# A decoder layer with expert choice: the threshold search split by batch, and the experts in a new order

## The reference

```
probs = softmax(einsum('bsd,ed->bse', x, choice_w), axis=-1)     # 8 experts
G, I = top_k(swapaxes(probs, -1, -2), k)                         # k = 256 of 1024 tokens
x_in = take_along_axis(x[:, None, :, :], I[..., None], axis=2)
h = silu(einsum('bekd,edf->bekf', x_in, w1))
x_mlp = einsum('bekf,efd->bekd', h, w2)
out[b, I] += G[..., None] * x_mlp      # then layernorm(x + out)
```

## Time and profile before

| | us |
| --- | --- |
| median of 3 runs | 1949.45 |
| lowest, highest | 1948.77, 1952.26 |
| the profiled execution's own time | 1959.72 |
| its span | 1957.9 |
| PE busy | 1668.1 |
| DVE busy | 1134.5 |
| ACT busy | 891.8 |
| POOL busy | 429.8 |

### The profile page before, as it was taken

The page is one execution under the profiler, slowest core; times in us unless marked ns, Lnnn a source line. Parts: engine busy times, 40 slices in busy tenths (PEclk is TensorE's granted clock), DMA queues, the critical chain, the costliest instruction groups (busy, mean ns, idle before and its releaser), DMA issues. The chain is left out here.

```text
span 1957.9 us, 32981 instructions
## 1 busy us (share of the span) xinstructions
PE 1668.1 (85%) x10632; PEld 848.3 (43%) x10632; DVE 1134.5 (58%) x1939; ACT 891.8 (46%) x1585; POOL 429.8 (22%) x547
## 2 busy tenths in 40 slices
PE   6599988798999888989998798999967844999993
PEld 3033334444332445433324354333245433888883
DVE  5577725756777256567763665677435366333424
ACT  2077773342777534347774343577833300111112
POOL 5200004302000052020001611100031001555563
PEclk9599999897999988979998899799988955999997
DMA  6700003622000044220000632200003040335446
GB/s 187 163 2 1 2 25 87 163 48 71 2 2 2 27 127 134 49 59 2 2 2 27 164 98 53 54 2 2 2 21 78 2 150 28 75 77 107 77 89 193
DMA packets 98037, 120.07 MB, mean 61 GB/s; under 512 B 17180, under 2 KB 73500, under 8 KB 97820
## 3 DMA queue, kind: packets, MB, share of 16 engines
q1 hardware_dynamic: 85468, 97.13, 18.1%
q0 software_dynamic: 12416, 20.98, 5.7%
HBM read 80.30 MB, written 40.79 MB: 62 GB/s over the span
## 5 line engine op out<-in xcount | busy, mean ns | idle before, releaser
L881 ACT ACTIVATE pT<-banks 128x512 f32<-128x512 f32 x1184 | 645.2, 596 | 254.8 <-PE banks L1492 150.0
L1034 DVE TENSOR_REDUCE nmf<-banks 128x1 f32<-128x1024 f32 x512 | 606.0, 1220 | 173.5 <-PE banks L1442 171.6
L1492 PE MATMUL banks<-qst,kst 99*128 99x512 bf16 x1024 | 344.0, 388 | 12.1 <-DVE nmf L1034 6.3
L1442 PE MATMUL banks<-kst,qst 96*128 96x512 bf16 x1024 | 327.0, 404 | 31.9 <-DMA kst<-k_parts 21.8
L1524 PE MATMUL banks<-pT,V 128*32 128x512 f32 x2048 | 273.8, 606 | 20.6 <-ACT oT L872 14.0
L1492 PEld LDWEIGHTS banks<-qst,kst 99*128 99x128 bf16 x1024 | 96.0, 97 | 307.2 <-ACT pT L881 185.8
L703 POOL CAST nmp<-nmf 128x16 bf16<-128x16 f32 x64 | 12.7, 198 | 831.4 <-DVE nmf L1034 516.6
L944 ACT ACTIVATE kst<-banks 128x512 f32<-128x512 f32 x64 | 38.2, 597 | 287.0 <-PE banks L1747 278.6
L1442 PEld LDWEIGHTS banks<-kst,qst 96*128 96x128 bf16 x1024 | 98.6, 100 | 146.4 <-DVE nmf L1034 37.3
L1029 DVE TENSOR_REDUCE nmf<-banks 128x4 f32<-128x616 f32 x128 | 99.6, 797 | 86.6 <-PE banks L1436 79.7
L1053 DVE RECIPROCAL rz<-banks 128x16 f32<-128x16 f32 x64 | 16.1, 251 | 204.5 <-PE banks L1552 203.4
(11 more groups left out here) (176 smaller groups left out, 2016.7 us busy)
## 6 DMA issues: line engine op xcount, KB each, us to landing
qst<-q_parts SPq DMA_DIRECT2D x48, 256.0 KB, 5.2
kst<-k_parts SPq DMA_DIRECT2D x48, 256.0 KB, 3.8
qst<-in_w SPq DMA_DIRECT2D x16, 512.0 KB
q_parts<-kst SPq DMA_DIRECT2D x48, 128.0 KB, 2.5
k_parts<-kst SPq DMA_DIRECT2D x48, 128.0 KB, 3.9
qx_parts<-kst SPq DMA_DIRECT2D x48, 128.0 KB, 3.1
qxs<-qx_parts SPq DMA_DIRECT2D x24, 256.0 KB, 5.0
qst<-qx_parts SPq DMA_DIRECT2D x24, 256.0 KB, 4.9
```

The costliest lines, as they stand in the source:

```text
L881: act.activation(pT[:, n % RING_P, :], PS[:, banks[what, n], :], ACT.Exp, scale=scale).then_inc(s_ex, 1)
L1034: dve.tensor_reduce(nmf[:, m % 2, j, t:t + 1], scores.rearrange("p a n -> p (a n)"), AX.X, ALU.max, negate=True).then_inc(s_smu, 1)
L1442: ins = pe.matmul(pair[:, half, :], qst[0:KQ, h, t * P:(t + 1) * P], kst[0:KQ, h, half * N:(half + 1) * N], start=True, stop=True)
L1492: ins = pe.matmul(ps, kst[0:KM, head, kc * P:(kc + 1) * P], qst[0:KM, head, cols], start=True, stop=True)
```

## The change

The search now belongs to a batch (8 columns instead of 32) and takes 3 bits in a turn, so 10 turns with 7 candidates each; a turn has one compare 448 wide, one product of PE with 448 columns (`count`), a reduction of it over the tiles from PSUM into `counts`, and the test and maximum as before. For batches 0 to 2 the ten counts stand in the tail of the next self-attention, one behind every fourth `st`; PSUM bank 3 is theirs, and the tail's scores have six banks instead of seven. In batch 3, `route_early` makes marks, ranks, the first three one-hots and the first tokens for the three batches between the first layernorm and cross-attention, while PE has the two rank steps among its query products and three picks behind them. POOL issues the first three gathers (six DMAs) behind the first `split_max` group of that cross-attention; three more picks stand in its tail. Weights 0 and 1 are loaded in that cross-attention.

The units are then: 24 for batches 0 to 2 (n = 3e + b), in whose first 12 the fourth batch's search and ranks are done, one step a unit; and 8 for batch 3, one expert each. There are three slots instead of four for gathered rows and results, so POOL issues gather n + 3 and scatter n; four weight buffers, with 16 loads instead of 8; `pick` and `choose` are six units ahead. The loops over experts are written out. SP stores each batch's layernorm twice, into `x2_rows` and `acc_rows`, and the four copies by POOL go. Sums of batches 0 to 2 are loaded from unit 24 on and their layernorms stand among units 26 to 29 (ACT's half up to 31). The diff, cut to what the text speaks of (`routing_open`, `routing_ties`, `picks_of` and `routing_places` do for a range of columns what the code before did for all 32; their bodies are left out):

```diff
-AT_ONCE = 2
+AT_ONCE = 3
 TRIES = 2 ** AT_ONCE - 1
 TURNS = BITS // AT_ONCE
 COLS = 5
-UNITS = 2 * B
+FINAL_FROM = 26
+EARLY = B - 1
+UNITS = B * E
+SLOTS = 3
+EARLY_PICKS = 2 * SLOTS
+WEIGHTS = 4
...
+def unit(n):
+    return (n // EARLY, n % EARLY) if n < EARLY * E else (n - EARLY * E, B - 1)
+def column(n):
+    e, b = unit(n)
+    return b * E + e
+def weights_of(n):
+    return n // EARLY if n < EARLY * E else E + n - EARLY * E
...
+COUNT_FROM, COUNT_EVERY = 3, 4
+COUNT_BANK = 3
...
+    last = max(n for n, (what, _) in enumerate(order) if what == "smax")
+    tail = [n for n, (what, _) in enumerate(order) if what == "st" and n > last]
+    at = {tail[COUNT_FROM + j * COUNT_EVERY]: j for j in range(TURNS)}
+    return [step for n, old in enumerate(order) for step in [old] + ([("count", at[n])] if n in at else [])]
+ORDER_NEXT = counts_in_tail([step for step in ORDER_SELF if step[0] != "smax" or step[1] >= AHEAD])
 ORDER_CROSS = schedule(SM_CROSS // NG, ST_CROSS // NG, 18, TURN_CROSS)
 
 
+LAST_MAX = ORDER_CROSS.index(("smax", SM_CROSS - 1))
+ORDER_LAST = (ORDER_CROSS[:LAST_MAX + 25] + [("pick", n) for n in range(SLOTS, EARLY_PICKS)]
+              + ORDER_CROSS[LAST_MAX + 25:])
...
+BANKS_NEXT, BEFORE_NEXT = score_banks(ORDER_NEXT, (0, 1, 2))
+BANKS_CROSS, BEFORE_CROSS = score_banks(ORDER_LAST, (0, 2, 3))
...
+                if not more:
+                    wait_apart(sp, s_pu, b * ST_ALL + ST_SELF)
+                    load_expert(0)
+                    load_expert(1)
...
+                for rows in (x2_rows, acc_rows):
+                    sp.dma_start(ROWS_P(rows[bass.ds(b * S, S), :]), z[:, :, :]).then_inc(s_x2, 16)
...
+            for w in range(WEIGHTS, 2 * E):
+                wait_apart(sp, s_y, last_unit(w - WEIGHTS) + 1 + START)
+                load_expert(w)
+                if w == E + WEIGHTS:
+                    for b in range(EARLY):
+                        load_sum(b)
...
+                split_max(b, SM_SELF, NG, SM_CROSS // NG, range(1 if not more else NG))
+                if not more:
+                    pool.wait_ge(s_x2, EARLY * 32 + START)
+                    pool.wait_ge(s_tk, 1)
+                    for n in range(SLOTS):
+                        gather(n)
+                    split_max(b, SM_SELF, NG, SM_CROSS // NG, range(1, NG))
...
-                pool.dma_start(acc_rows[rows, :], x2_rows[rows, :]).then_inc(s_sc[b], COPIED)
...
+            for n in range(UNITS):
+                e, b = unit(n)
+                if n + SLOTS < UNITS:
+                    if n + SLOTS == EARLY * E:
+                        pool.wait_ge(s_x2, B * 32 + START)
+                    wait_apart(pool, s_tk, (n + SLOTS) // SLOTS * 2 + 1, s_gt, n + 1 + START)
+                    gather(n + SLOTS)
+                wait_apart(pool, s_tk, n // SLOTS * 2 + 2, s_ye, n + 1 + START,
+                           *([s_sc[b], e * 32] if e else []))
+                scatter(n)
+                if FINAL_FROM <= n < FINAL_FROM + EARLY:
+                    last_rsqrt(n - FINAL_FROM)
+            last_rsqrt(B - 1)
...
+            def radix_open(link_r):
+                link_r(dve.tensor_tensor(cand[:, :, :].bitcast(I32),
+                                         thr[:, :].bitcast(I32).rearrange("p (j n) -> p j n", j=1)
+                                         .to_broadcast([P, TRIES + 1, E]), step[:, :, :].bitcast(I32), ALU.bitwise_or))
+                dve.tensor_tensor(reached[:, :, :, :],
+                                  probB[:, :, :].rearrange("p t (j n) -> p t j n", j=1).to_broadcast([P, T, TRIES, E]),
+                                  cand[:, 1:, :].rearrange("p (t j) n -> p t j n", t=1)
+                                  .to_broadcast([P, T, TRIES, E]), ALU.is_ge).then_inc(s_in, 1)
+                dve.tensor_scalar(step[:, :, :].bitcast(I32), step[:, :, :].bitcast(I32), AT_ONCE, None,
+                                  ALU.logical_shift_right)
+            def radix_close(link_r, bank, made):
+                dve.wait_ge(s_cn, made)
+                dve.tensor_reduce(counts[:, :], PS[:, bank, 0:T * TRIES * E].rearrange("p (t k) -> p k t", t=T),
+                                  AX.X, ALU.add).then_inc(s_cr, 1)
+                dve.wait_ge(s_cr, made)
+                link_r(dve.scalar_tensor_tensor(out=cand[:, 1:, :],
+                                                in0=counts[:, :].rearrange("p (j n) -> p j n", n=E),
+                                                scalar=float(CAP), in1=cand[:, 1:, :], op0=ALU.is_ge, op1=ALU.mult))
+                link_r(dve.tensor_reduce(thr[:, :], cand[:, :, :].rearrange("p j n -> p n j"), AX.X, ALU.max))
...
+                radix_begin(link_b)
+                for j in range(TURNS):
+                    radix_open(link_b)
+                    radix_close(link_b, COUNT_BANK, b * TURNS + j + 1)
+                link_b(dve.tensor_copy(thr_all[:, bass.ds(b * E, E)], thr[:, :]))
...
+            def route_early(b):
+                made[0] = EARLY * RADIX_STEPS
+                dve.wait_ge(s_pu, b * ST_ALL + ST_SELF)
+                cols, done = slice(0, EARLY * E), EARLY * TURNS
+                routing_open(cols)
+                picks_of(cols)
+                routing_ties(cols, done + 1)
+                routing_places(cols, done + 2)
+                for n in range(SLOTS):
+                    choose(n)
+                take_choice(0)
+                scatter_tokens(0)
...
+            cols, done = slice(EARLY * E, BE), EARLY * TURNS + 2
+            turned(0)
+            turned(1)
+            radix_begin(link_r)
+            for n in range(UNITS):
+                q, k = divmod(n, SLOTS)
+                if n + 2 < UNITS:
+                    turned(n + 2)
+                if n < TURNS:
+                    radix_open(link_r)
+                elif n == TURNS:
+                    link_r(dve.tensor_copy(thr_all[:, cols], thr[:, :]))
+                    routing_open(cols)
+                if n + EARLY_PICKS < UNITS:
+                    choose(n + EARLY_PICKS)
+                if n < TURNS:
+                    radix_close(link_r, 0, done + n + 1)
+                elif n == TURNS:
+                    picks_of(cols)
+                    routing_ties(cols, done + n + 1)
+                elif n == TURNS + 1:
+                    routing_places(cols, done + n + 1)
+                gated(n)
+                if k == SLOTS - 1 and (q + 1) * SLOTS < UNITS:
+                    scatter_tokens(q + 1)
+                    if (q + 2) * SLOTS < UNITS:
+                        take_choice(q + 2)
+                if FINAL_FROM < n <= FINAL_FROM + EARLY:
+                    apply_layernorm(n - FINAL_FROM - 1)
+                if FINAL_FROM <= n < FINAL_FROM + EARLY:
+                    last_statistics(n - FINAL_FROM)
+            last_statistics(B - 1)
+            apply_layernorm(B - 1)
...
+                    elif what == "count":
+                        if n == 0:
+                            pe.wait_ge(s_smu, b * SM_ALL + SM_SELF)
+                        count(COUNT_BANK, (b - 1) * TURNS + n + 1)
+                    elif what == "pick":
+                        pick(n)
...
+            def count(bank, made):
+                pe.wait_ge(s_in, made)
+                pe.matmul(PS[:, bank, 0:T * TRIES * E], onesb[:, :],
+                          reached[:, :, :, :].rearrange("p t j n -> p (t j n)"),
+                          start=True, stop=True).then_inc(s_cn, 1)
...
+                    if not more and i == 1:
+                        rank_ties(EARLY * E, EARLY * TURNS + 1)
+                    elif not more and i == 2:
+                        rank_chosen(EARLY * E, EARLY * TURNS + 2)
...
+                if not more:
+                    for n in range(SLOTS):
+                        pick(n)
+                    pe.wait_ge(s_cr, EARLY * TURNS + 2)
...
+            turn_rows(0)
+            turn_rows(1)
+            hidden(0)
+            for n in range(UNITS):
+                if n + 2 < UNITS:
+                    turn_rows(n + 2)
+                if n + 1 < UNITS:
+                    hidden(n + 1)
+                if n < TURNS + 2:
+                    pe.wait_ge(s_te, n + 3 + START)
+                if n < TURNS:
+                    count(0, done + n + 1)
+                elif n == TURNS:
+                    rank_ties(E, done + n + 1)
+                elif n == TURNS + 1:
+                    rank_chosen(E, done + n + 1)
+                if n + EARLY_PICKS < UNITS:
+                    pick(n + EARLY_PICKS)
+                expert_out(n)
```

More of the change, by code:

```diff
@@ L308, in room @@
             return k_room[:, used[0] - words:used[0]]
-        xg = [room(2 * D).rearrange("p (j d) -> p j d", d=D) for _ in range(B)]
+        BE = B * E
+        picks = room(T * BE * 6 // 2).bitcast(BF16).rearrange("p (t n k) -> p t n k", n=BE, k=6)
+        pos = room(T * BE).rearrange("p (t n) -> p t n", n=BE)
+        above, equal, chosen = [room(T * BE // 2).bitcast(BF16) for _ in range(3)]
```

(50 more changed lines are left out.)

462 lines of the change are left out of this document (194 added, 268 removed).

## The result

The changed kernel takes 1931.28 us (median of 4 runs, 1926.57 to 1933.49) beside 1949.66 us for the kernel before (1948.77 to 1952.26): ratio 0.990, interval 0.988 to 0.9921. Run again in another set it gave 1931.25 us, ratio 0.9904 (0.9887 to 0.992). The direction was right; 20 us of the forecast gain are missing, and the time lies 0.3 us above the 1931 at which the stated range ends.

A forecast was written before the change was run, and what follows sets the result against it. It took an 84.44 us hole before the experts as the room to gain, with PE bounding the experts. Eight terms, chiefly -75.5, +18 and +12, summed to -38.2 us, giving 1911 us as median; range 1892 to 1931.

The forecast's parts named there:

- step 3: Last expert units: sum loads of batches 0 to 2 make one or two gathers late, +2 us, bounds 0 and 4.4.
- the second store: Storing x2 twice by SP, 1 MB more each batch: nothing, at most 2.8 us if minus-max rows queued behind.
- Step 5: Three self-attention tails: PE waits for each of ten search turns on DVE, +12 us, bounds 0 and 24.
- Step 1: Hole between the last batch's logits and the experts: search and first gathers move out of it, -75.5 us.
- Step 2: Pace of the experts: with three slots, gathers behind scatters land late and PE waits every second unit, +18 us.
- Rival D: Slower than before: gathers held by the scatter in front and weight loads, experts 62 us more, 1973 us; chance 0.03.
- Step 4: End of the kernel, last scatter and sum load after PE's end: -3 us, bounds -5 and 0.
- Step 6: Batch 3 before cross-attention: routing fits DVE's idle time, only ranks on PE delay, +0.8 us, bounds 0 and 3.5.
- Step 7: Batch 3's cross-attention: six gathers on POOL delay the second maxima split and PE, +4.5 us, bounds 0 and 7.9.
- Step 8: Last cross tail: three picks on PE, the third waiting for its one-hot, +3 us, bounds 0 and 5.
- Rival C: Both delays larger: search turns of 2.96 us and gathers landing 0.6 later, +11 and +8, 1930 us; chance 0.18.
- Profile and median: Whole kernel: profiled 1959.72 less 38.2 gives 1921.5; the runs' median taken as 10.3 below, so 1911 us.

The follow-up runs named there:

- The gather kernel: The changed kernel with POOL issuing gather n+4 ahead of scatter n, where it was behind it: 1902.91 us, ratio 0.9743.
- the kernel with all loads last: The changed kernel with early layernorms moved behind unit 31 and the three sum loads behind the output of unit 29: 1925.47 us, ratio 0.986.

## Why the prediction was off, by its own steps

The forecast had the signs and the order of the terms right, and two things in it failed: step 3 and the zero for the second store. Step 5 was half right. In the pair of profiles the sum reads -38.2 forecast and -26.2 measured (1959.72 to 1933.49).

- **Step 1**, -75.5: right. The same half clock and the same steps behind the copy; from the logits to iteration 0 nothing was lost.
- **Step 2**, +18: right in mechanism, and in size partly by luck. Up to 1840.45 the units took 227.8 us; the working gives 229.2. The waits did not stand in every second unit, as the prediction wanted, but in 22 of 25, with 0.3 to 1.9 us each. Two errors met: P was 7.83 and not 8.35, as a pick costs 0.54 in the unrolled code, and the gather chain was 10.04 (a pair of 17.87 less 7.83) and not 9.85. From the start of the second issue the gather took 2.87 us, where the prediction had 2.52 from the traffic row. The Trainium skill's rule (DMA: Bandwidth & Descriptors, Anatomy of one DMA), counted from the end of the issue as the prediction did, gives an estimate of 3.3, too much by about as much as the row was too little. Rival D did not come: no gather waited for a scatter's landing before the last units. The gather kernel shows that nearly the whole term came from one place in a queue.
- **Step 3**, +2: failed. The rest of the units took 63.3 us against 53.9 forecast without this term: +9.4. The bound of 4.4 took one gather late beside the loads; there were two stalls, 4.50 and 6.43 us, and behind each the clock fell, so that sixteen hidden products took 5.31 and 5.62 us instead of 3.62. Part of the second is a wait that the sum had no term for: the early layernorm, with POOL's power ahead of a gather, 2.3 us. The prediction had asked only whether DVE's 4.4 us had room.
- **Step 4**, -3: right, -3.6.
- **Step 5**, +12: the turn was right (2.56 to 2.60 us, counts that far apart), the price not. It is 2.8, 2.8 and 2.5 in the three tails, 8.1 in all: the 2.07 us of the earlier trace rows is a tail's fastest burst and was taken for its mean. The unrolled turns show no 0.40 of idle between them, only 0.35 to 0.54 before the reduction, for the count itself. That agrees with the Trainium skill's rule on branches (Runtime: NRT & Kernel Launch, Instruction fetch mechanics); no run tells it from another cost of the loop.
- **Step 6**, +0.8: +0.4. **Step 7**, +4.5: 6.3, since the first gather waits 0.67 and takes 1.23, and six take 7.5 us from first to last; the reading that PE leads and gives nothing back was right. **Step 8**, +3: 4.0.
- **The second store**, 0, with 2.8 as its bound: failed. PE's wait for the minus-max rows went from 0.33 to 3.22 us in batch 1, and the first group of maxima was split 3.65, 3.0 and 2.8 us later against the store in the three batches. The rows of 4 KB that PE needs next stand behind the megabyte; with the store asked for later the wait is gone. Some of the delay returned elsewhere: up to batch 3's first layernorm the shift was 15.8 us, made of 9.5 (three stores), 8.1 (three tails), 0.95 before them and 1.3 ahead of that layernorm, less 1.9 in each of two middle stretches (a remainder of 0.3 is left); what gave it back was not examined.
- **Profile and median.** The working took 10.3 us off the profiled execution, as it lay above the median before. After the change it lies 2.2 above. Those 8 us are in no step: one execution is a draw, and its distance to the median does not carry over.

So of the 20 us, 12 are in steps (7.4 in step 3, 3.8 up to batch 3's layernorm, 2.8 in steps 7 and 8, less 2 in the others) and 8 in the conversion. Rival C reached the same 1930 by other causes. Its turns of 2.96 us were no longer than the 2.6 forecast, and of its 0.6 us of later landing 0.35 came, which the shorter P made good. That the time came out near the range's end is so no credit to the sum.

## What to carry to other kernels

In an engine's queue a prefetch belongs ahead of the write-back it doesn't depend on: with a slot less it was some 30 us, for an exchange of two lines. When a transfer or a small operation is added, list what small, urgent thing is issued next in the same queue, and who waits for it; megabytes in front of 4 KB and a power in front of a gather were the two errors here. A pace read from one burst is a lower bound: take the mean over the stretch, boundaries in it, before pricing what is put between.

## What was not expected of the hardware

PE's granted clock can make a wait dearer than it looks. After 1.93 us of waiting for a gather, sixteen products took 5.31 us with the clock down to 1.2 GHz, although PE had been busy till then. In the kernel with all loads last, the same wait was followed by 3.62 (the second pair of rows):

```profile
1631.03 0.66 PE L1849 MATMUL banks<-ident,kst 128*128 128x128 f32 x4 [1.93 <-DMA kst<-x_rows,tok_g]
1631.52 5.31 PE L1862 MATMUL banks<-kst,qst 128*128 128x256 f32 x16
...
1633.09 0.66 PE L1847 MATMUL banks<-ident,kst 128*128 128x128 f32 x4 [1.87 <-DMA kst<-x_rows,tok_g]
1633.58 3.62 PE L1860 MATMUL banks<-kst,qst 128*128 128x256 f32 x16
```

In this place four runs waited 1.91 to 1.95 us and fell to 1.2 GHz, five waited 1.84 to 1.89 and did not. Yet near the end of four kernels with the gather ahead, waits of 2.09, 2.16 and 2.30 us were followed by full clock and one of 2.28 by the lower one. So the length of the wait alone does not tell, and one unit can differ by 1.7 us between two kernels that are the same up to there. And a wait removed gave next to nothing in one batch, where the clock came back 9.4 us behind the first scores instead of 4.0. A gather landed 2.8 us from the start of its issue in the quiet stretch and in 4.8 to 6.7 in the two stalls, beside the loads near the end; a scatter in 3.9 and in 7.2 to 7.9.
